# One more drain of GpSimd between its two groups of scatters, in an attention and mixture-of-experts kernel

## The chip, the cores and the metric

The kernel runs on one core of one Trainium2 chip. The metric is the device time of one execution in microseconds (us); the time before is the median of three executions. One further execution was recorded by the hardware profiler, and all rows below come from that one.

Engines are called PE (TensorE matmul), PEld (TensorE weight load), DVE (VectorE), ACT (ScalarE), POOL (GpSimd) and SP (SyncE). A name with a q behind it, such as POOLq, is the sequencer of that engine, which takes the instructions in order and hands them on.

## The reference, cut to what matters

A block with adaptive layer norm: a gated attention-like layer on 8 x 512 tokens of width 128, then a router that sends each token to one of 16 experts. Every expert takes at most 320 tokens. What matters here is the second half:

```python
    h = _layernorm(x, axis=-1) * (1 + cb) + sb
    # _L0_ffn_ref(h, gate_w, w1, w2):
    tokens = x.reshape(-1, D_MODEL)
    capacity = _capacity(s, N_EXPERTS)                       # 320
    gate_logits = tokens.astype(jnp.float32) @ gate_w.T
    combine_weights, sec_mask = _top1_router(gate_logits, capacity)
    dispatch = jnp.einsum('sec,sd->ecd', sec_mask.astype(tokens.dtype), tokens)
    h = jax.nn.gelu(jnp.einsum('ecd,edf->ecf', dispatch, w1))
    expert_out = jnp.einsum('ecf,efd->ecd', h, w2)
    out = jnp.einsum('sec,ecd->sd', combine_weights.astype(tokens.dtype), expert_out)
    # and behind it
    x = x + gb * out
```

## The kernel before

Every engine has its own instruction list, written out by hand in one block, and the engines wait for each other by semaphores. The program has two stages.

**The first stage** runs over 8 batches of 512 tokens (`b` is 0 to 7). Each batch goes through the attention layer, gives rows of `x1` and of the normed `h2`, and gets a slot number per token from the router. GpSimd takes part with three elementwise functions (`squares`, `weigh_sums`, `silu`), with `count_seen`, and with `scatter(b)`. That last one issues four indirect DMAs (line L417), one for each 128 tokens. Each moves 128 rows of 386 floats from the tile `rows` to the DRAM tensor `dispatched_rows`, at the rows that the slot numbers name. There are 32 of them in all, here called the dispatch scatters. They raise the semaphore `scattered`, by 16 each.

**The second stage** runs over 8 pairs of experts. When `scattered` has reached its full value, SP loads the first experts' rows (`hin`), and DVE, after the same wait, makes the low halves of the first two weights (`w1l`, L882, two instructions) and then those of the rows (`xtl`, L888 and L891). TensorE multiplies (L1180 with the first weights, L1194 with the second), turns the results back (L1158), and DVE weighs them and adds `x1` (L904 and L912, which write a part of `x_all` that is called `fin`). `send_tiles` on GpSimd then waits for `fin_done` and issues an indirect DMA for each 128 rows (L439) to the output. There are 40 of those, here called the result scatters, five for each pair of experts; the last pair's come in a group of two and a group of three.

**The end.** SP waits for all result scatters to land (`final_out`, L369). After that every engine's list ends in an instruction that the block adds, a DRAIN at L63, followed by a meeting of all engines. A DRAIN is a sequencer's instruction that holds the sequencer until its engine has nothing left to do. The program also has such a DRAIN on each engine at its very start (L1247). Between the two, no engine's list has one.

Of the kernel before, what the change touches and what calls it, by code (L numbers as in the profile page):

```python
# [5 lines left out]
def adaln_attention_moe(  # L6
# [35 lines left out]
    NB, T, D = x_d.shape  # L42
    NJ = T // P
    NTOK = NB * T
    NE, _, FF = w1_d.shape
    NF = FF // P
    CAP = int(1.25 * NTOK / NE)
# [15 lines left out]
    with ctx:  # L63
# [3 lines left out]
        def sem(name):  # L67
            return ctx.enter_context(nc.semaphore(name))
# [168 lines left out]
        x1_out, scattered = sem("x1_out"), sem("scattered")  # L237
# [135 lines left out]
        def _(pool):  # L373
# [55 lines left out]
            scatter(4); count_seen(5); scatter(5); count_seen(6); scatter(6); scatter(7)  # L429

            pool.wait_ge(x1_out, 16 * NB)

            last_token = pool.to_reg(NTOK - 1)

# [825 lines left out]
```

## Time and profile before

| what | us |
|---|---|
| median of three executions | 222.36 |
| lowest and highest of them | 222.19 and 223.55 |
| the profiled execution's own time | 221.95 |
| span in the profile, from first to last instruction | 220.2 |
| TensorE busy | 186.2 |
| VectorE busy | 153.3 |
| ScalarE busy | 150.9 |
| GpSimd busy | 101.5 |

The span leaves out what lies before the first and behind the last instruction, 1.75 us in the profiled execution. The granted clock of TensorE was 0.949 of full speed over the span. Busy times of sequencer instructions such as DRAIN are not in the busy times of the engines.

### The profile page before, as it was taken

The page shows a single profiled execution, that of the slowest core. Times are in us where ns is not written, and L with a number is a line of the kernel's source. Part 1 is how long each engine was busy: PE and PEld are TensorE (multiplying, and loading weights), DVE is VectorE, ACT ScalarE, POOL GpSimd, SP SyncE. Part 2 cuts the span into 40 slices and gives each one's busy share as a digit, 9 for nine tenths or more (in the row PEclk, how much of TensorE's full clock was granted, in tenths as well). Part 3 has the DMA queues.
Part 4 walks back from the last instruction along what each step waited for, and adds up shares of the span by engine and source line. Part 5 has one row for each costly group of instructions (what it writes and reads, how often), then busy time and mean ns, then how long its engine had stood idle before and what let it go on. Part 6 is the DMA issues. An engine that isn't in the chain of part 4 may idle for free.

```text
span 220.2 us, 3901 instructions
## 1 busy us (share of the span) xinstructions
PE 186.2 (85%) x1128; PEld 149.4 (68%) x1128; DVE 153.3 (70%) x478; ACT 150.9 (69%) x438; POOL 101.5 (46%) x115
## 2 busy tenths in 40 slices
PE   7979989998998999698657779999999999999300
PEld 5858678687875988666445437788888887887100
DVE  3799799999999899999873244376684774836400
ACT  5398999999999999986562906558576485643000
POOL 6130132442046347656886520007466485474770
PEclk9999999999999999999995599999999999999855
DMA  5999999991104113412552229999977854110010
GB/s 143 290 347 358 360 351 327 335 263 58 48 3 151 47 48 127 158 53 79 183 194 83 78 77 304 358 355 323 322 228 218 287 160 149 33 42 12 24 37 0
DMA packets 37284, 38.60 MB, mean 175 GB/s; under 512 B 2591, under 2 KB 31334, under 8 KB 37264
## 3 DMA queue, kind: packets, MB, share of 16 engines
q1 hardware_dynamic: 33936, 31.29, 45.5%
q0 software_dynamic: 3328, 7.07, 9.0%
q8 instruction: 9, 0.15, 0.3%
q14 instruction: 11, 0.09, 0.1%
HBM read 19.19 MB, written 18.95 MB: 173 GB/s over the span
## 4 chain that ended last, share of the span: by engine, by line
PE 57%; DVE 16%; ACT 11%; issue 7%; POOL 4%; DMA 1%; POOLq 1%; DVEq 0%; ACTq 0%
PE bank L1194 16%; PE bank L1180 13%; PE bank L962 5%; ACT junk L476 3%; ACT ewkv L495 3%; PE bank L1063 2%; PE bank L1158 2%; PE bank L1014 2%; POOL dispatched_rows L417 2%; DVE w1l L882 2%; POOL out_dram L439 2%; PE bank L979 2%; PE bank L1151 2%; PE bank L1031 2%; PE bank L1000 2%
## 5 line engine op out<-in xcount | busy, mean ns | idle before, releaser
L439 POOL DMA_INDIRECT out_dram<-x_all,rest x40 | 42.2, 1054 | 43.4 <-DVE x_all L912 34.0
L417 POOL DMA_INDIRECT dispatched_rows<-rows,slot x32 | 31.5, 985 | 17.0 <-DVE slot L800 8.5
L1194 PE MATMUL bank<-HT,w 128*128 128x320 f32 x128 | 37.0, 432 | 0.0
L637 ACT ACTIVATE HT<-bank 128x320 f32<-128x320 f32 x64 | 28.0, 439 | 9.4 <-PE bank L1180 9.0
L1194 PEld LDWEIGHTS bank<-HT,w 128*128 128x128 f32 x128 | 23.5, 189 | 7.6
L1180 PE MATMUL bank<-xth,w1h 128*128 128x320 f32 x64 | 22.9, 358 | 0.3 <-DVE xtl L888 0.3
L924 DVE COPY OT<-bank 128x320 f32<-128x320 f32 x16 | 7.9, 492 | 21.9 <-PE bank L1194 21.9
L882 DVE TENSOR_TENSOR w1l<-w,w1h 128x1024 fp32r<-128x1024 f32 x8 | 16.2, 2028 | 6.9 <-DMA dispatched_rows<-rows,slot 6.9
L1180 PE MATMUL bank<-xth,w1l 128*128 128x320 f32 x64 | 19.8, 309 | 0.0
L1180 PE MATMUL bank<-xtl,w1h 128*128 128x320 f32 x64 | 19.8, 309 | 0.0
L476 ACT ACTIVATE junk<-bank 128x128 f32<-128x128 f32 x64 | 16.6, 291 | 2.6 <-PE bank L962 2.6
L399 POOL TENSOR_TENSOR hsq<-hT 128x512 f32<-128x512 f32 x8 | 9.5, 1187 | 17.9 <-ACT hT L468 16.6
L495 ACT ACTIVATE ewkv<-bank,nrr 128x128 f32<-128x128 f32 x64 | 17.4, 381 | 0.2
L275 POOL TENSOR_TENSOR yT<-kvsum,rden 128x512 f32<-128x512 f32 x7 | 8.9, 1277 | 17.1 <-ACT rden L507 10.8
L609 ACT CAST w1h<-w 128x1024 fp32r<-128x1024 f32 x8 | 16.3, 2044 | 0.0
L962 PE MATMUL bank<-wqkvT,hT 128*128 128x256 f32 x64 | 15.5, 384 | 0.7 <-ACT ewkv L495 0.3
L622 ACT CAST xth<-bank 128x640 fp32r<-128x640 f32 x7 | 4.8, 692 | 15.8 <-PE bank L1151 15.8
L1014 PE MATMUL bank<-diag_ga,hT 128*128 128x128 f32 x64 | 12.9, 283 | 3.3 <-DVE GT L729 3.2
L979 PE MATMUL bank<-ident,ewkv 128*128 128x128 f32 x96 | 13.8, 275 | 0.7 <-ACT ewkv L495 0.7
L476 ACT ACTIVATION_READ_ACCUMULATOR junk<-bank 128x1 f32 x64 | 14.3, 223 | 0.0
L962 PEld LDWEIGHTS bank<-wqkvT,hT 128*128 128x128 f32 x64 | 11.6, 190 | 3.5 <-issue 1.9
L537 ACT ACTIVATE xh<-rows,nm,rs 128x128 f32<-128x128 f32 x32 | 13.2, 495 | 0.8 <-DVE nm L754 0.8
(161 smaller groups left out, 458.9 us busy)
## 6 DMA issues: line engine op xcount, KB each, us to landing
w<-in_L_ffn_w_dram SPq DMA_DIRECT2D x16, 512.0 KB, 8.3
dispatched_rows<-blank SPq DMA_DIRECT2D x8, 965.0 KB, 12.6
rest<-dispatched_rows SPq DMA_DIRECT2D x8, 645.0 KB, 6.4
hin<-dispatched_rows SPq DMA_DIRECT2D x7, 320.0 KB, 7.7
x_all<-in_L_attn_x_dram SPq DMA_DIRECT2D x8, 256.0 KB, 5.1
rows<-gb_row SPq DMA_DIRECT2D x8, 256.0 KB, 5.9
out_dram<-rows SPq DMA_DIRECT2D x8, 256.0 KB
out_dram<-x_all,rest POOLq DMA_INDIRECT x40, 3.0
```

The source lines that it names most:

```text
L417: pool.indirect_dma_start(out=disp_d, out_offset=bass.IndirectOffsetOnAxis(ap=slot[:, b, j:j + 1], axis=0), in_=rows[:, b, j, :], in_offse ...
L439: pool.indirect_dma_start(out=out_d.rearrange("b t d -> (b t) d"), out_offset=bass.IndirectOffsetOnAxis(ap=rest[i % RING][:, n, C_TOK - D: ...
L476: last = act.activation(junk[:, 2 * j + m, :], ps_qk[:, j, m * D:(m + 1) * D], ACT.Square, accum_out=ssq[:, j, m:m + 1])
L495: last = act.activation(t[:, j, m, :], ps_qk[:, j, m * D:(m + 1) * D], ACT.Exp, scale=nrr[:, 2 * j + m:2 * j + m + 1])
L609: act.copy(w1h[i % 2][:, :, :, :], w1[i % RING][:, :, :].rearrange("p e (m f) -> p e f m", f=NF)).then_inc(w1h_done, 1)
L637: act.activation(HT[e][:, f, :], ps_h[c % HB][:, 0:CAP], ACT.Gelu_apprx_tanh).then_inc(h_done, 1)
L882: dve.tensor_tensor(w1l[i % 2][:, :, :, :], w1[i % RING][:, :, :].rearrange("p e (m f) -> p e f m", f=NF), w1h[i % 2][:, :, :, :].bitcast( ...
L962: last = pe.matmul(ps_qk[:, j, :], hT[b % NHT][:, j * P:(j + 1) * P], wqkvT[:, 0:2 * D], start=True, stop=True)
L979: last = pe.transpose(ps[:, j * P:(j + 1) * P], t[:, j, m, :], ident[:, :])
L1014: pe.matmul(ps_u[:, j * P:(j + 1) * P], hT[b % NHT][:, j * P:(j + 1) * P], diag_ga[:, b, :], start=True, stop=False)
L1180: last = pe.matmul(ps_h[c % HB][:, 0:CAP], w[i % 2][:, e, f, :], x[i % 2][:, e * CAP:(e + 1) * CAP], start=(n == 0), stop=(n == 2))
L1194: last = pe.matmul(ps_o[e], w2[i % RING][:, e, f, :], HT[e][:, f, :], start=(f == 0), stop=(f == NF - 1))
```

## The change

Behind the last dispatch scatter, GpSimd's list gets two instructions: a wait until all 32 dispatch scatters have landed, and a drain. Nothing is removed and nothing changes its place; the other engines' lists stay as they are.

```diff
@@ -429,6 +429,8 @@
             scatter(4); count_seen(5); scatter(5); count_seen(6); scatter(6); scatter(7)
 
             pool.wait_ge(x1_out, 16 * NB)
+            pool.wait_ge(scattered, 16 * NB * NJ)
+            pool.drain()
 
             last_token = pool.to_reg(NTOK - 1)
 
```

## Rows read from the trace of the kernel before

**Rows 1.** The page: shares of the chain that ended last, by engine.

```profile
PE 57%; DVE 16%; ACT 11%; issue 7%; POOL 4%; DMA 1%; POOLq 1%; DVEq 0%; ACTq 0%
```

**Rows 2.** The chain from 201 us on: start us, us, what.

```profile
207.15 0.57 DVE x_all L912
...
207.91 0.97 POOL out_dram L439
208.88 0.30 issue
...
213.01 0.97 POOL out_dram L439
```

**Rows 3.** Instructions of L63: duration ns min/median/max, first and last start us.

```profile
L63 POOLq EVENT_SEMAPHORE  x2: 17/17/17, 220.0 to 220.1; - x2
L63 ACTq DRAIN  x1: 468/468/468, 202.4 to 202.4; - x1
L63 DVEq DRAIN  x1: 597/597/597, 207.2 to 207.2; - x1
L63 POOLq DRAIN  x1: 10692/10692/10692, 209.2 to 209.2; - x1
```

**Rows 4.** The last ACT and DVE instructions, timeline from 201 us on.

```profile
202.38 0.44 ACT L637 ACTIVATE HT<-bank 128x320 f32<-128x320 f32 x1 [2.16 <-PE bank L1180]
...
207.15 0.56 DVE L912 TENSOR_TENSOR x_all<-junk,rest 128x384 f32<-128x384 f32 x1
```

**Rows 5.** Instructions of L1247, at the start of the program.

```profile
L1247 DVEq DRAIN  x1: 10/10/10, 0.1 to 0.1; - x1
...
L1247 POOLq DRAIN  x1: 188/188/188, 0.4 to 0.4; - x1
L1247 POOL MEMSET const-uint8-127<- x1: 118/118/118, 0.4 to 0.4; 128x1 uint8 x1
```

**Rows 6.** SP's end of waiting, instructions of L369.

```profile
L369 SPq EVENT_SEMAPHORE  x2: 17/22/28, 208.7 to 215.1; - x2
```

**Rows 7.** Groups of instructions on POOL: busy us, mean ns, idle before.

```profile
L439 POOL DMA_INDIRECT out_dram<-x_all,rest x40 | 42.2, 1054 | 43.4 <-DVE x_all L912 34.0 <-issue 9.4
L417 POOL DMA_INDIRECT dispatched_rows<-rows,slot x32 | 31.5, 985 | 17.0 <-DVE slot L800 8.5 <-issue 7.0 <-ACT rows L552 1.2
```

**Rows 8.** Timeline, all engines, 127 to 148 us: where the two groups of scatters meet.

```profile
127.44 0.97 POOL L417 DMA_INDIRECT dispatched_rows<-rows,slot  x1 [0.30 <-issue]
...
129.62 0.37 SPq L350 DMA_DIRECT2D hin<-dispatched_rows  x1
129.63 3.93 DVE L882 TENSOR_TENSOR w1l<-w,w1h 128x1024 fp32r<-128x1024 f32 x2 [6.88 <-DMA dispatched_rows<-rows,slot]
...
133.47 0.49 DVE L888 TENSOR_TENSOR xtl<-bank,xth 128x320 fp32r<-128x320 f32 x1
...
134.01 0.41 PE L1180 MATMUL bank<-xth,w1h 128*128 128x320 f32 x1 [0.30 <-DVE xtl L888]
...
146.46 0.82 DVE L912 TENSOR_TENSOR x_all<-junk,rest 128x640 f32<-128x640 f32 x1
...
148.14 0.97 POOL L439 DMA_INDIRECT out_dram<-x_all,rest  x1 [19.72 <-DVE x_all L912]
```

**Rows 9.** Timeline of POOL, then of DVE, around 152 us.

```profile
151.97 0.97 POOL L439 DMA_INDIRECT out_dram<-x_all,rest  x1 [0.30 <-issue]
153.25 1.59 POOL L439 DMA_INDIRECT out_dram<-x_all,rest  x1 [0.30 <-issue]
...
152.00 2.03 DVE L882 TENSOR_TENSOR w1l<-w,w1h 128x1024 fp32r<-128x1024 f32 x1
```

**Rows 10.** All eight instructions of L882: duration ns min/median/max.

```profile
L882 DVE TENSOR_TENSOR w1l<-w,w1h x8: 1996/2034/2042, 129.6 to 187.7; 128x1024 fp32r<-128x1024 f32 x8
```

**Rows 11.** GpSimd's DMA queue, 60 to 130 us and 147 to 220 us: packets, MB, share.

```profile
q0 software_dynamic: 2048, 5.30, 20.6%
...
q0 software_dynamic: 1280, 1.77, 7.3%
```

## The prediction

> **What bounds the kernel now.** I read the chain that ended last first. TensorE has 57% of it and GpSimd only 4% with another 1% for its sequencer [rows 1], so on the whole this is a TensorE kernel, and an instruction more on GpSimd looks irrelevant. The end of that chain tells something else. DVE finishes the last result at 207.15 + 0.57 = 207.7 us; from there on GpSimd works alone, five result scatters at a pitch of 0.97 + 0.30 = 1.27 us, the last one from 213.01 to 213.98 [rows 2]. But the span ends at 220.2 us. Chain rows stop at 213.98, so I looked at what the sequencers do after it, the instructions of L63. The reader is to see the closing DRAIN of GpSimd: it starts at 209.2, when its sequencer has handed on all scatters, and takes 10.692 us, to 219.9; the meeting of the engines is at 220.0 to 220.1 [rows 3]. So GpSimd's closing drain sets the end of the program.
>
> How long should such a drain be? On ACT it ends at 202.4 + 0.47 = 202.87, and the last ACT instruction ends at 202.38 + 0.44 = 202.82; on DVE it ends at 207.8 and the last instruction at 207.71 [rows 3, 4]. That is 0.05 to 0.1 us behind the last work. GpSimd's own first drain, at the start of the program, takes 0.188 us from 0.4, to about 0.6, where the memset in front of it ends at about 0.5: again 0.1 us [rows 5]. The closing one ends 219.9 - 213.98 = 5.9 us behind the last scatter. Waiting for data doesn't explain it: SP sees the last result landed at 215.1 [rows 6], and the drain goes on for 219.9 - 215.1 = 4.8 us more. What stands between GpSimd's first drain and its last are 32 + 40 = 72 scatters [rows 7]. So a drain after scatters has 5.9 - 0.1 = 5.8 us of work that a drain without them hasn't.
>
> **The change, part by part.** It removes and moves nothing. Two instructions are added.
>
> The wait for the dispatch scatters: SP and DVE wait for the same semaphore value and go on at 129.62 and 129.63 [rows 8], so GpSimd passes it then too. It had its last dispatch scatter out at 127.44 + 0.97 = 128.4 and has nothing to do until the first result is ready at 146.46 + 0.82 = 147.3 [rows 8]. Behind the new wait on GpSimd stand only the result scatters. Cost: nothing, with 147.3 - 129.6 = 17.7 us of cover.
>
> The drain: its own length isn't in the trace of before. From below it is the 0.1 us of a drain without scatters [rows 5], from above the 5.8 us that the closing drain does behind 72 scatters. Both lie within the 17.7 us. Should it be longer than these, it costs only what goes beyond 17.7 us, and even then first on GpSimd's list: the first result scatter of 148.14 would be late, and four more stand behind it before the next group.
>
> What it gives at the end depends on what the 5.8 us are made of. If they are bookkeeping for every scatter since the last drain, each costs 5.8 / 72 = 0.081 us, the new drain does 32 x 0.081 = 2.6 us of it in the idle stretch, and the closing one keeps 0.1 + 40 x 0.081 = 3.3 us. It then ends at 213.98 + 3.3 = 217.3, later than the landing at 215.1, so the landing does not hold it. This **2.6 us** is the value I take: it counts from the end of the last instruction, and there the other engines' drains end, within 0.1 us [rows 3, 4].
>
> Bounds around it. If the drain first waits for the landing at 215.1 and works then, 4.8 us are shared by 72: 0.067 each, and the gain is 32 x 0.067 = 2.1 us. If the work goes by packets, not by scatters, GpSimd's queue moved 2048 in the stretch of the dispatch scatters and 1280 in that of the results [rows 11], 62% in the first, and the gain is 0.62 x 5.8 = 3.6 us. Going by bytes, 5.30 of 7.07 MB [rows 11], it would be 75%, 4.3 us; a length of rows seems an unlikely thing for bookkeeping to depend on, so I take 3.6 for the upper end. From below, nothing, or a loss, as in the rivals.
>
> A row against a rule: the starting drains are short here, 10 ns on DVE [rows 5], and the closing one of GpSimd is 10,692 ns. The Trainium skill, Vector Engine: DVE Perf Modes, section "The DRAIN you can't avoid", says that the drains in the opening and closing of a program are about 12 ns, constant, on all engines. By that rule there is nothing to save and the time stays at 222.4. DVE's starting drain agrees, GpSimd's closing one doesn't.
>
> **Sum.** Profiled execution: span 220.2 - 2.6 = 217.6, own time 221.95 - 2.6 = 219.35. The median of the runs is 222.36, 0.41 above the profiled one; 222.36 - 2.6 = 219.8 us, 1.2% less.
>
> **Rivals.**
>
> *The closing drain has a fixed length after scatters* (or its work covers only the latest of them). One look at a queue's state, with the same price after 40 scatters as after 72, would also give 0.1 us at the start and 5.9 at the end. For it speaks that two drains can't tell a slope from a step; against it, that 5.8 us is long for one look. The new drain then costs 5.8 us out of sight, and the closing one stays at 5.9. Time: 222.4 us.
>
> *The new drain does nothing of that work.* It is a sequencer's instruction; it may only wait for the engine to be idle, which at 129.6 it has long been, and the bookkeeping may belong to the program's end alone. For it: GpSimd was done at 128.4, so such a drain has nothing to wait for. Against it: no row shows two kinds of drain. Time: 222.4 us.
>
> *The new drain gets in DVE's way.* It starts at 129.6, just when DVE starts the two `w1l`, 3.93 us, behind which stand `xtl` and the first matmul of the experts at 134.01 [rows 8]: without any slack, every us there is one at the end. GpSimd and DVE do hinder each other: the scatter of 153.25 took 1.59 us in place of 0.97, and ended 0.8 us behind a `w1l` that ran from 152.00 to 154.03 [rows 9]; the group's mean of 1054 ns against 985 carries five such cases [rows 7]. If the drain holds what both need, for a fixed 5.8 us, and gives nothing back at the end, the time is 222.36 + 5.8 = 228.2 us. It decides for slower as soon as it holds DVE 2.2 us longer than it saves. If it holds DVE for the 2.6 us that it then saves, the two cancel: 222.4. Against both: it is always GpSimd that waited. The `w1l` of 152.00 began while a scatter ran since 151.97, and took 2.03 us like the rest of the eight, 1996 to 2042 ns [rows 9, 10].
>
> The Trainium skill, SBUF — State Buffer, section "SBUF: two separate sides", calls the port that the two share an exclusive lock, held by whichever starts first for its whole instruction, which is the rule by which this rival could win. Here only the direction from DVE to GpSimd shows.
>
> **How the numbers follow.** A measurement of this kernel can tell about 1%, 2.2 us, from no change. Work that goes by what was scattered since the last drain: 64%, with 2.1 to 3.6 us gained; its own range is 218.7 to 220.4. Of it I put 46 points beyond 2.2 us, since both 2.6 and 3.6 are, and 18 within. Fixed length: 20%. No such work in the new drain: 7%. Blocking that cancels the gain: 2%. Blocking that costs: 5%, and 2% for something else that makes it slower. So faster 0.46, same 0.18 + 0.20 + 0.07 + 0.02 = 0.47, slower 0.07. The range must take in the cases without change, or it would leave out three in ten: from 222.36 - 3.7 = 218.7 up to 222.36 + 0.3 = 222.7, the 0.3 for the scatter of medians.
>
> **What would show it.** In the profile after, GpSimd's list has a DRAIN that starts at about 129.6 and takes some 2.7 us; `w1l` still starts at 129.6 and takes 3.9; the first result scatter still comes 0.9 us behind the first result; and the closing drain ends 3.3 us behind the last scatter. A new drain of 5.9 us and a closing one still 5.9 behind the last scatter is the fixed length. A new drain of 0.1 us or less with nothing changed at the end is the second rival. A `w1l` pair that starts late or takes longer than 3.93 is the third. The prediction is wrong if the closing drain's 5.9 us don't follow the number of scatters since the last one, or if something that I don't see, such as the latest result scatters alone, makes them.

## The result and the profile after

The changed kernel is faster: the ratio of its time to the kernel before is 0.9874, 95% interval 0.9844 to 0.9905, from twenty executions of each; applied to the 222.36 us of before that is 219.6 us, where 219.8 was forecast. Both kernels also had slower executions (up to 228.1 us before; up to 225.6 and one of 478.0 after), and those more than 1.5% above the fastest of the same kernel are left out of every ratio here.

The page after, its first and chain lines, against [rows 1]. The short chain share of PE only says that the trace was followed back less far.

```profile
span 218.3 us, 3903 instructions
...
PE 39%; DVE 9%; issue 3%; POOL 3%; ACT 2%; DMA 1%; POOLq 1%; ACTq 0%
```

The new drain, instructions of line L433 (duration ns min/median/max, first and last start us):

```profile
L433 POOLq DRAIN  x1: 2680/2680/2680, 130.5 to 130.5; - x1
```

The end of the chain after (start us, us, what), against [rows 2]:

```profile
207.94 0.57 DVE x_all L914
...
208.70 0.97 POOL out_dram L441
209.68 0.30 issue
...
213.82 0.97 POOL out_dram L441
```

The closing instructions, L63, against [rows 3]:

```profile
L63 POOLq EVENT_SEMAPHORE  x2: 17/17/17, 218.2 to 218.2; - x2
...
L63 DVEq DRAIN  x1: 595/595/595, 208.0 to 208.0; - x1
L63 POOLq DRAIN  x1: 8087/8087/8087, 210.0 to 210.0; - x1
```

The sums: the last scatter ends at 213.82 + 0.97 = 214.8, the closing drain at 210.0 + 8.087 = 218.1, 3.3 us later; before, it was 5.9 by the rounded rows (5.96 unrounded). The new drain takes 2.680 us, and it took exactly that in each of the nine profiles here that have it behind 32 landed scatters. What left the end came back in the idle stretch.

That stretch, timeline after, against [rows 8]:

```profile
128.20 0.98 POOL L417 DMA_INDIRECT dispatched_rows<-rows,slot  x1 [0.30 <-issue]
...
130.39 3.94 DVE L884 TENSOR_TENSOR w1l<-w,w1h 128x1024 fp32r<-128x1024 f32 x2 [6.89 <-DMA dispatched_rows<-rows,slot]
...
134.80 0.41 PE L1182 MATMUL bank<-xth,w1h 128*128 128x320 f32 x1 [0.23 <-DVE xtl L890]
...
148.93 0.97 POOL L441 DMA_INDIRECT out_dram<-x_all,rest  x1 [19.75 <-DVE x_all L914]
```

The drain, 130.5 to 133.2, lies wholly beside the two `w1l`, which take 3.94 us where they took 3.93, and wholly within GpSimd's idle time. The first result scatter starts 18.5 us behind the start of `w1l`, as before (148.14 - 129.63 = 18.5).

The span fell by 1.9 us and not by 2.6, because in this execution the second stage begins 0.8 us later (130.39 against 129.63). That cannot be the drain's doing, since it starts only at 130.5. The windows view shows what goes with it (us; busy us and instructions of PE, PEld, DVE, ACT, POOL; granted clock; DMA share; GB/s), first before, then after:

```profile
60.00:129.00 69.00, 56.28 (x385) 43.19 (x383) 53.63 (x198) 54.66 (x163) 42.15 (x45) 0.93 0.28 97
```

```profile
60.00:129.00 69.00, 57.32 (x385) 44.31 (x383) 53.95 (x198) 54.88 (x164) 41.96 (x45) 0.90 0.28 97
```

The granted clock of TensorE from 60 to 129 us, a mean over time at 2.4 and at 1.2 GHz, was 0.93 before and 0.90 after, and TensorE was busy 1.0 us longer there for the same 385 instructions; another execution of the changed kernel (the last one of it below) had 0.87 there and started `w1l` at 132.1. A measure that doesn't depend on the first stage is the time from DVE's last instruction to the end of the span: 220.2 - 207.7 = 12.5 us before, 218.3 - 208.5 = 9.8 after, 2.7 less.

### The profile page after: what moved, and what is told of

Read it like the earlier page. It is cut to its first block, busy times and chain, and to the rows that moved or that the text cites. A ratio compares the mean times of both kernels' runs of the same rounds, so it can differ in the third digit from the quotient of the medians.

```text
span 218.3 us, 3903 instructions
## 1 busy us (share of the span) xinstructions
PE 187.8 (86%) x1128; PEld 150.1 (69%) x1128; DVE 153.1 (70%) x478; ACT 150.9 (69%) x438; POOL 101.6 (47%) x115
## 4 chain that ended last, share of the span: by engine, by line
PE 39%; DVE 9%; issue 3%; POOL 3%; ACT 2%; DMA 1%; POOLq 1%; ACTq 0%
PE bank L1196 16%; PE bank L1182 13%; PE bank L1160 2%; PE bank L1033 2%; DVE w1l L884 2%; POOL out_dram L441 2%; PE bank L1153 2%; PE bank L1041 1%; DMA dispatched_rows<-rows,slot 1%; PE bank L1007 1%; POOL dispatched_rows L417 1%; PE bank L1026 1%; ACT h2T L549 1%; ACT xh L539 1%; DVE gc L725 1%
## 5 line engine op out<-in xcount | busy, mean ns | idle before, releaser
L981 PE MATMUL bank<-ident,ewkv 128*128 128x128 f32 x96 | 14.3, 281 | 0.7 <-ACT ewkv L497 0.7
## 6 DMA issues: line engine op xcount, KB each, us to landing
dispatched_rows<-blank SPq DMA_DIRECT2D x8, 965.0 KB, 12.5
```

Of the source, the lines that this page charges most:

```text
L981: last = pe.transpose(ps[:, j * P:(j + 1) * P], t[:, j, m, :], ident[:, :])
```

## The experiments

**The wait alone.** The changed kernel without its drain.

```diff
             pool.wait_ge(scattered, 16 * NB * NJ)
-            pool.drain()
```

> The changed kernel without its drain: only the added wait for the dispatch scatters stays. If the drain does the work (my theory), nothing is gained: the closing drain ends 5.9 us behind the last result scatter as in the kernel before, and the ratio to the kernel before is 1.00. If it is the wait that gives the time (GpSimd or its queue being better off once the landings are known), the closing drain ends 3.3 us behind and the ratio is 0.988.

Its last scatter and its closing drain (timeline, and instructions of L63):

```profile
224.73 0.97 POOL L440 DMA_INDIRECT out_dram<-x_all,rest  x1 [0.30 <-issue]
```

```profile
L63 POOLq DRAIN  x1: 11082/11082/11082, 220.6 to 220.6; - x1
```

The drain ends at 231.7, the last scatter at 225.7: 6.0 us, as before the change (5.96 unrounded in both). The median was 235.75 us of four runs against 233.15 of before; on that chip single runs of before went from 229.3 to 239.1, so the time decides nothing there, the row does. The wait gives nothing.

**The drain without the wait.**

```diff
+            pool.drain()
             pool.wait_ge(x1_out, 16 * NB)
-            pool.wait_ge(scattered, 16 * NB * NJ)
-            pool.drain()
```

> The drain stands directly behind the last dispatch scatter, with no wait for the landings. Theory A, the work of a drain starts with the end of the last scatter and doesn't wait for data: the new drain ends 2.7 us behind the last dispatch scatter, and the closing one 3.3 us behind the last result scatter, ratio 0.988 as with the wait. Theory B, a drain first waits for the data to land (1.2 us behind the scatter) and works then, or bookkeeping covers only what has landed: the new drain ends 3.5 to 3.9 us behind the scatter, or is shorter and leaves one to three scatters' 0.08 us each to the closing one. In both the ratio stays within 0.002 of 0.988, since the stretch is idle.

```profile
138.55 0.97 POOL L417 DMA_INDIRECT dispatched_rows<-rows,slot  x1 [0.30 <-issue]
...
140.73 3.92 DVE L883 TENSOR_TENSOR w1l<-w,w1h 128x1024 fp32r<-128x1024 f32 x2 [6.87 <-DMA dispatched_rows<-rows,slot]
```

```profile
L430 POOLq DRAIN  x1: 5825/5825/5825, 136.4 to 136.4; - x1
```

The new drain ends at 142.2, 2.7 us behind the last dispatch scatter (139.5), though the data landed only at 140.7, when DVE goes on. So the 2.7 us run from the scatter's end, and the landing adds nothing to them: theory A for these 32 scatters. With fewer of them it does add something, as the drains further down show. The closing drain (220.3 + 8.471 = 228.8, last scatter 225.5) ends 3.3 us behind, so the added wait isn't needed for the gain. The median, 233.02 us of four runs, lies in the same spread as that of before and says nothing.

**Half the rows.** Result scatters of 64 rows, 40 of them as ever; half of the result rows are left out of the output, so this kernel is only for reading the rows.

```diff
-    ap=rest[i % RING][:, n, C_TOK - D:C_TOK - D + 1].bitcast(i32), axis=0),
-  in_=fin[i % RING][:, n, :], ...
+    ap=rest[i % RING][0:P // 2, n, C_TOK - D:C_TOK - D + 1].bitcast(i32), axis=0),
+  in_=fin[i % RING][0:P // 2, n, :], ...
```

> The changed kernel with result scatters of 64 rows in place of 128 (half of the result rows are left out of the output); still 40 of them. If the drain's work goes by scatters, the closing drain still ends 3.3 us behind the last one. If it goes by rows (one descriptor for each), it ends 0.1 + 40 x 0.04 = 1.7 us behind. The new drain after 32 full dispatch scatters stays at 2.7 us in both.

```profile
225.29 0.91 POOL L441 DMA_INDIRECT out_dram<-x_all,rest  x1 [0.30 <-issue]
```

```profile
L63 POOLq DRAIN  x1: 8627/8627/8627, 220.9 to 220.9; - x1
```

220.9 + 8.627 = 229.5 against 226.2: 3.3 us. The new drain stays at 2.680. The price goes by scatters, not by rows.

**Doses.** Three drains in the first half: one behind the first 24 dispatch scatters, whose landing is not waited for, one behind the 8 others, and one directly behind that, with no DMA between.

```diff
-            scatter(4); count_seen(5); scatter(5); count_seen(6); scatter(6); scatter(7)
+            scatter(4); count_seen(5); scatter(5); pool.drain(); count_seen(6); scatter(6); scatter(7)
...
             pool.wait_ge(scattered, 16 * NB * NJ)
             pool.drain()
+            pool.drain()
```

> The changed kernel with a drain behind dispatch batch 5 (24 scatters so far, not waited for), the drain behind all landed dispatch scatters (8 more since), and a second one right behind that (none since). By 0.1 us and 0.081 us a scatter: the first ends 2.0 us behind its last scatter, the second takes 0.75 us, the third at most 0.1. If a drain's price were fixed once scatters have run, the second and third would take 2.7 us like the one drain of the changed kernel; if a drain always goes through all scatters of the program, 2.7 each as well. The closing drain stays at 3.3 us in all.

```profile
L429 POOLq DRAIN  x1: 6475/6475/6475, 125.2 to 125.2; - x1
...
L433 POOLq DRAIN  x1: 707/707/707, 145.6 to 145.6; - x1
...
L434 POOLq DRAIN  x1: 46/46/46, 146.4 to 146.4; - x1
```

8 scatters cost 707 ns, none 46 ns, and the 32 of the changed kernel 2680. That is (707 - 46) / 8 = 82.6 ns a scatter, and (2680 - 707) / 24 = 82.2 ns. Fixed prices are out. The line 0.046 + 0.0824 x n gives 3.34 us for 40 and 5.98 for 72, where 3.33 and 5.96 were measured; the closing drain of this run has 3.3 too. The forecast of the first of these drains missed: it ended at 131.7, 3.0 us behind its last scatter (128.7) in place of 2.0. It is the only one of the three whose scatters hadn't landed when its turn came. The last semaphore update that the trace has from them is at 130.6, and the sum of the prices would end at 130.7 as well, so waiting for the landing alone doesn't explain 131.7; the table behind the last experiment does.

**Plain DMAs.** Eight plain DMAs of a small tile, then a drain.

```diff
+        spare_out = sem("spare_out")
...
             pool.drain()
+            spare_d = nc.dram_tensor("spare", [8, P, 32], i32, kind="Internal").ap()
+            for k in range(8):
+                pool.dma_start(spare_d[k, :, :], tokid[:, :]).then_inc(spare_out, 16)
+            pool.wait_ge(spare_out, 16 * 8)
+            pool.drain()
```

> The changed kernel with eight plain DMAs of a small tile to a spare DRAM tensor issued by GpSimd in its idle stretch, behind the new drain, then a wait for them and one more drain. If the price belongs to every DMA that GpSimd issues, that drain takes 0.05 + 8 x 0.082 = 0.7 us; if it belongs to indirect scatters alone, 0.05 us. The new drain stays at 2.7 us, the closing one at 3.3 us behind the last scatter.

```profile
L439 POOLq DRAIN  x1: 706/706/706, 142.9 to 142.9; - x1
```

706 ns, to one nanosecond the drain behind eight scatters; the closing drain again ends 3.3 us behind the last scatter. The price belongs to each DMA that GpSimd issues, of either kind.

**A drain behind each of six result groups.** If 40 scatters can be worked off in gaps, the closing drain should shrink further.

```diff
             for i in range(LAST):
                 send_tiles(i, i, 0, NS)
+                if i < LAST - 1:
+                    pool.drain()
```

> The changed kernel with six more drains, one behind each of the first six groups of five result scatters; ten result scatters are left for the closing drain. At 0.081 us for each scatter and 0.1 for the drain, each of the six takes 0.5 us behind its last scatter and fits into GpSimd's idle 2.16 us. The closing one would need 0.9 us, but the last data lands 1.1 to 1.2 us behind the last scatter, so the landing becomes the bound: the program ends some 1.3 us behind the last scatter, 2 us sooner than in the changed kernel and 4.6 sooner than before, ratio 0.979. If the closing drain's 3.3 us are a fixed price after any scatter, it stays 3.3 and the ratio 0.988. If drains in the middle wait for landings and so hold back the next group of scatters, or hold DVE's weights (w1l over 2.05 us), the ratio is above 0.985.

The ratio was 1.0027, interval 0.9955 to 1.0099: the whole gain is gone. The forecast failed, its third case (drains that hold back the next group) came true, and the rows say where. The six drains, and the closing one:

```profile
L451 POOLq DRAIN  x6: 5861/6867/9593, 159.9 to 209.7; - x6
```

```profile
L63 POOLq DRAIN  x1: 9792/9792/9792, 220.6 to 220.6; - x1
```

Scatters of POOL around the first drain and the last one of all, with the idle time before each:

```profile
163.30 1.58 POOL L441 DMA_INDIRECT out_dram<-x_all,rest  x1 [0.30 <-issue]
170.31 0.97 POOL L441 DMA_INDIRECT out_dram<-x_all,rest  x1 [5.43 <-issue]
...
227.85 0.97 POOL L441 DMA_INDIRECT out_dram<-x_all,rest  x1 [0.30 <-issue]
```

The closing drain did shrink: 220.6 + 9.792 = 230.4, 1.6 us behind the last scatter (228.8). But the first group's drain ended at 159.9 + 9.593 = 169.5, 4.6 us behind its last scatter, not 0.5, and the next scatter came 0.8 us after that. The DMA view of 158 to 170 us shows the queue of SP on all engines just then (packets, MB, share of 16 engines):

```profile
q1 hardware_dynamic: 3494, 3.66, 95.0%
```

The same group's scatters in the changed kernel land late, those of the last groups don't (time from a scatter's start until its semaphore update, windows 148 to 155 and 201 to 215 us):

```profile
DMA to landing us min/median/max: 4.1/5.1/6.2
```

```profile
DMA to landing us min/median/max: 2.1/2.2/2.2
```

In the version with six drains the last semaphore update of the first group comes at 169.2, and the drain ends at 169.48, 0.25 us behind it; each of the five drains after it ends 0.24 us behind the last update of its group. So a drain also holds GpSimd until its DMAs have landed, and a little longer. Behind six such drains the last scatter ends at 228.8, 11.0 us behind DVE's last instruction (217.8) instead of the 6.3 us of the changed kernel (214.8 - 208.5). 4.7 lost there and 1.7 won at the closing drain leave 3 us more than the changed kernel: 12.8 us from DVE's end to the end of the span (230.6 - 217.8), nearly the 12.5 of before.

**One drain, behind group 5; two drains, behind groups 3 and 5.** The edits are as above, with `if i == LAST - 2:` and `if i in (LAST - 4, LAST - 2):`. The changed kernel ran beside them.

> The changed kernel as it is, timed beside the next ones on their chip. Ratio to the kernel before 0.988 (2.6 us of 222), new drain 2.7 us, closing drain 3.3 us behind the last scatter.

> The changed kernel with one more drain, behind result group 5. It handles 30 scatters, 2.5 us behind the last one, where the gap has 2.0 of slack: the last two groups are 0.5 us late, the closing drain is 1.4 to 1.6 as above. So 1.2 us less than the changed kernel, ratio 0.982.

> The changed kernel with two more drains, behind result groups 3 and 5 (of 0 to 7). The runs so far say: a drain ends when both are done, 0.1 us and 0.08 us for each scatter since the last drain, counted from the last scatter's end, and the landing of that scatter, 1.4 us behind its end where DMA traffic is light. Behind group 3 it handles 20 scatters: 1.7 us. With 0.8 us until the next scatter starts, that is 0.3 to 0.4 us late, and the next gap has 1.3 us of slack for it. Behind group 5 it handles 10, so the landing sets 1.4 us, and the gap there has 2.0. The closing one handles 10, and ends 1.4 to 1.6 us behind the last scatter in place of 3.3. So 1.7 to 1.9 us less than the changed kernel, ratio to before 0.980. If a drain in this stage always puts off the groups behind it (as all six did together), the last scatter is 1 us or more later against DVE's last instruction than the 6.3 us of before, and the ratio is 0.985 or more.

On this chip the changed kernel had a ratio of 0.9896, interval 0.9848 to 0.9945, and the version with two drains 0.9812, interval 0.9714 to 0.9911. The changed kernel's profile has the expected drains, 2.680 us and 3.3 us behind the last scatter. In the profile of the version with two drains the closing one ends at 225.59 + 7.643 = 233.2, 1.6 us behind the last scatter (231.6), and the one behind group 3 ends 2.1 us behind its scatter (200.4 against 198.3), where 1.7 was forecast. The version with a single drain came to no ratio, its times (median 233.94 us of six, the lowest 229.63) being too spread. Its profile, scatters and then the drain:

```profile
209.22 0.97 POOL L441 DMA_INDIRECT out_dram<-x_all,rest  x1 [0.30 <-issue]
213.53 0.97 POOL L441 DMA_INDIRECT out_dram<-x_all,rest  x1 [3.34 <-issue]
```

```profile
L451 POOLq DRAIN  x1: 6587/6587/6587, 206.1 to 206.1; - x1
```

The drain over 30 scatters ends at 212.7, 2.5 us behind the scatter, as forecast; DVE's result had been ready at 212.0, so the next group is some 0.7 us late. From DVE's last instruction to the end of the span it is 227.8 - 218.65 = 9.2 us, against 228.0 - 217.8 = 10.2 in the changed kernel's profile on that chip: 1.0 us less by the rows, where 1.2 was forecast.

Both intervals of the pair being wide, it was run again on another chip.

> The changed kernel once more, beside the version with two more drains: ratio to the kernel before 0.988.

> The version with drains behind result groups 3 and 5 once more. By its first profile the closing drain ends 1.6 us behind the last scatter in place of 3.3, and the first scatter of group 6 isn't late: 1.7 us less than the changed kernel, ratio to before 0.980. If the two drains put off the last two groups (as the single one behind group 5 did, by some 0.8 us), the ratio is 0.984.

The changed kernel: 0.9858, interval 0.9803 to 0.9914, median 220.72 us. Two more drains: **0.9761**, interval 0.9693 to 0.983, median 218.35 us. The profile of the latter, the gap behind group 3, the last scatter, the drains of the groups and the closing one:

```profile
180.43 1.65 POOL L441 DMA_INDIRECT out_dram<-x_all,rest  x1 [0.31 <-issue]
185.02 0.97 POOL L441 DMA_INDIRECT out_dram<-x_all,rest  x1 [2.95 <-issue]
...
202.02 0.97 POOL L441 DMA_INDIRECT out_dram<-x_all,rest  x1 [2.79 <-DVE x_all L916]
...
213.50 0.97 POOL L441 DMA_INDIRECT out_dram<-x_all,rest  x1 [0.30 <-issue]
```

```profile
L451 POOLq DRAIN  x2: 5657/6426/7195, 177.0 to 195.2; - x2
```

```profile
L63 POOLq DRAIN  x1: 6316/6316/6316, 209.7 to 209.7; - x1
```

The drain behind group 3 ends at 184.2, 2.1 us behind its scatter (1.7 was forecast), and makes the next group a little late; by group 6 (202.02) that is made up, since the scatter waits for DVE again, with the same 2.79 us of idle time as in the changed kernel. The closing drain ends at 216.0, 1.6 us behind the last scatter (214.5; 1.57 unrounded), which lands at 213.5 + 2.2 = 215.7. From DVE's last instruction to the end it is 216.3 - 208.2 = 8.1 us, against 9.8. On both chips this version's ratio is some 0.9 points below the changed kernel's; the two intervals overlap each time, so the size of the step rests on the rows, 1.7 us, and its sign on rows and both pairs.

**When a drain ends.** The runs above leave misses of one kind: behind 5, 10, 20 and 24 scatters a drain ends later than both its sum of prices and the landing. The unrounded times of the traces give a rule for it. "Landed" is the last semaphore update by a DMA that the trace has from the scatters before the drain (part of these updates is missing in some traces); all times are in us from the span's start.

| drain | scatters since the last drain | last scatter ends | landed | drain ends | behind the landing |
|---|---|---|---|---|---|
| six drains, first | 5 | 164.88 | 169.23 | 169.48 | 0.25 |
| six drains, third | 5 | 187.82 | 188.96 | 189.20 | 0.24 |
| two drains again, closing | 10 | 214.48 | 215.61 | 216.05 | 0.44 |
| two drains again, behind group 3 | 20 | 182.07 | 183.33 | 184.19 | 0.86 |
| doses, first | 24 | 128.66 | 130.62 | 131.65 | 1.03 |
| behind group 5 alone | 30 | 210.19 | 211.32 | 212.70 | 1.38 |
| without the wait | 32 | 139.53 | 140.71 | 142.22 | 1.51 |
| changed kernel, closing | 40 | 214.79 | 215.92 | 218.12 | 2.20 |
| before, closing | 72 | 213.98 | 215.12 | 219.94 | 4.82 |

One rule fits all nine within 0.02 us: half of the price, 0.041 us a DMA, is worked off from the last scatter's end; then the drain waits for the landing, if that is later; then come the other half and the 0.046. For 20 scatters the first half is done at 182.07 + 0.82 = 182.89, the landing at 183.33 holds the drain, and 183.33 + 0.82 + 0.05 = 184.20, where 184.19 was measured. For 40 the first half ends at 214.79 + 1.65 = 216.44, behind the landing, and nothing is held: 216.44 + 1.65 + 0.05 = 218.14, measured 218.12. Of the 26 drains here that began before their DMAs had landed it fits 25 to 0.02 us; the other is 0.15 us off, and its trace has only three updates behind the last scatter. A drain that begins behind the landing, like the new one, runs both halves at a stretch. The rule was found in runs made for other questions; no run was made to test it, and what the two halves are isn't shown.

## Why the prediction was right

*The closing drain sets the end, and 5.8 us of it are work for the 72 scatters.* Right. By doses it is 0.0824 us a scatter, where 0.081 was worked out, and 0.046 us for a drain with none, where 0.1 was.

*The new drain costs nothing.* Right by the rows: 2.680 us from 130.5, "some 2.7" forecast, in a stretch of 17.7 us.

*The gain, 32 x 0.081 = 2.6 us.* Right: the closing drain ends 3.3 us behind the last scatter, down from 5.9, and 1.26% of the time is gone (0.95 to 1.56% by the interval) against 1.2% forecast. That the landing does not hold the closing drain is right for its 40 scatters, but by 0.5 us only: the first half of the work ends at 216.4, the landing is at 215.9. With a landing 1.14 us behind the last scatter, an estimate from the table puts the border at 1.14 / 0.041, some 28 scatters. Of the bounds, the lower (all work after the landing, 2.1 us) falls with the drain that had no wait: 2.7 us from the scatter's end, not from the landing 1.2 us later. The upper one (by packets, 3.6 us) falls with the price: dispatch scatters, 64 packets each by [rows 11], cost 0.082 us, and result scatters, 32 each, cost (3.3 - 0.05) / 40 = 0.081.

*Rivals.* The fixed length and the drain that does nothing are out by the new drain's 2680 ns and by the doses 707 and 46. Blocking DVE is out: the drain ran beside `w1l` and that took 3.94 us. The rule of the Trainium skill (SBUF — State Buffer, "SBUF: two separate sides") of an exclusive lock did not bite from the drain's side; GpSimd's scatters went on being the ones that wait, as the one of 163.30 in the version with six drains, 1.58 us in place of 0.97 beside a `w1l` that ran from 162.06 to 164.09. The other rule of the Trainium skill, of drains of about 12 ns at the ends of a program (VectorE: DVE Perf Modes, "The DRAIN you can't avoid"), agrees with DVE's at the start, 10 ns [rows 5]. The page speaks of the drains that the runtime puts around a kernel, and those here are instructions of the kernel's own program, so it says nothing on them that these runs could refute. GpSimd's took 46 ns with no DMA since the last drain, and 8.1 to 11.1 us at the end of the kernels without result drains.

The recorded range, 218.7 to 222.7, takes in no change at all, so that the time lies in it says little; the rows and the 219.8 are what came true. Its lower end is also 0.1 too low for its own sum, 222.36 - 3.6 = 218.8. The chances were too even. Nearly half lay on "same", though the row of a 0.188 us drain and the row of a 10.7 us one left little but the scatters between them. What I hadn't reasoned out is what the experiments with later drains then ran into: a drain waits for the landing as well, and works off half of its price only behind it, which costs nothing only where the engine is idle for long enough or the scatters since the last drain are many.

## What to carry to other kernels

Look at what the sequencers do behind the last row of the chain. Where GpSimd issues DMAs, its drain at the end takes 0.08 us for each one since its last drain; a drain in a stretch where GpSimd is idle for long enough takes that off the end of the program. Before one is put into a short gap, its end is to be worked out: the later of the landing in that gap and 0.04 us a DMA behind the last issue, then 0.04 us a DMA once more. The next scatter started 0.8 us behind that.

## What the runs showed that was not expected

- The price is the same for a plain DMA of 16 KB and an indirect scatter of 128 rows: 706 and 707 ns for eight.
- It is linear from 0 to 72 DMAs where the landing doesn't hold it (46, 707, 2680 ns, and 3.33, 5.96 us behind the last scatter). Where it does, the drain ends half of the price behind the landing: 0.25 us for 5, 0.44 for 10, 0.86 for 20, 1.03 for 24.
- The landing of a scatter that takes 2.2 us on nearly idle DMA engines takes up to 6.2 us beside SP's loads, and with five scatters a drain there ended 4.6 us behind the last of them.
